# The empty slots of the late expert table moved from its end to its front

## The chip, the cores and the metric

The kernel runs on one core of one Trainium2 chip. Times are device microseconds (us) of one launch. The kernel before takes 1703.07 us, the median of 3 runs (1702.03 to 1703.34). Everything read from a trace comes from one profiled execution.

Names of engines: PE is TensorE, ACT is ScalarE, DVE is VectorE, POOL is GpSimd, SP is SyncE, which only issues DMAs here. Each engine works through its own instructions in order and waits on semaphores.

## The reference, cut to what matters

One decoder layer on x [8, 512, 256], float32: a linear attention, a causal cross attention with 16 heads, and a mixture of 16 experts with the best 4 for each token. The change touches only the last part:

```
def _L0_ffn_ref(hidden_states, router_w, router_b, w1, b1, w2, b2):
    logits = hidden_states @ router_w + router_b
    probs = jax.nn.softmax(logits, axis=-1)
    topw, topi = jax.lax.top_k(probs, 4)
    topw = topw / jnp.sum(topw, axis=-1, keepdims=True)
    combine = jnp.sum(jax.nn.one_hot(topi, 16) * topw[..., None], axis=2)
    ...
    def body(acc, expert):                      # 16 experts
        hmid = jax.nn.gelu(x @ w1e + b1e, approximate=False)
        return (acc + (hmid @ w2e + b2e) * ce[:, None], None)
x = x + _L0_ffn_ref(_layernorm(x), ...)
```

4096 tokens with 4 experts each are 16384 pairs, spread very unevenly over the 16 experts.

## The kernel before, in words

The kernel sorts the pairs by expert in DRAM (`expert_rows`, one region for each expert; a row is the normalised token, its id and its gates) and computes tiles of 256 rows of one expert. How many tiles an expert needs is known only at run time, so the program has a fixed number of slots, `MOE_TILES` = 79, the most that can ever be needed, and a table says for each slot j which expert owns it (`owner`), at which row it starts (`first_row`) and on which earlier slots its output must wait (`landed`).

The table comes in two parts. The first 24 slots (`SURE_TILES`) take full tiles from the first six batches. The other 55 (`LATE_TILES`) are laid out when all tokens are routed: `count_tiles` gives the late tiles of each expert and their running sum `cum`; `find_owners` gives slot n (the column `number`, one slot per partition) the expert whose sums enclose n; `find_rows` turns that into a row and into the two flags `meets`. For the inputs of the reference, counting its routing gives 49 late tiles, for experts 0 to 15:

```
2 1 1 2 1 1 3 1 4 6 1 9 1 1 1 14
```

so 6 of the 55 late slots are empty. An empty slot is computed like any other, on the padding rows that stand behind expert 0's last row; their ids point to 256 spare rows behind the real output. Before the change the real tiles are slots 24 to 72 and the empty ones 73 to 78.

What a slot does, in the order of `attention_plan` (in round j: `turn_x` of j+1, `load_x` of j+3, `hidden` of j, `split_w1` of j+2, `load_w1` of j+4, `results` of j-1):

- SP loads the 256 rows (`load_x`, L1702) and the expert's w1 (`load_w1`, L1721).
- PE transposes the rows (L1739), makes the hidden layer (24 matmuls, L1757) and the results (24 matmuls, L1772).
- DVE copies ids and gates of the rows to `tail` (L1837), of which there are 5 buffers (`NT`): for slot j+1 it first waits until the output of slot j-4 has landed. Behind it stands the low half of the transposed rows (L1839), without which PE can't begin the hidden layer of j+1.
- ACT scales the result with the gate and writes it to `y` (L1805), of which there are 3 buffers (`NY`): it waits until the output of slot j-3 has landed.
- POOL adds the result to the output in DRAM: two indirect DMAs of 128 rows with `compute_op=ADD` (L1874). Two adds in flight must not touch the same output row. Tiles of one expert never do, tiles of two experts can. So POOL waits, before the adds of slot j, for the landing of slot j-1 if j is the first tile of its expert (in this part of the table), and for the landing of slot j-2 if j is its first or second (`meets`, L200; the waits are L1870). From the third tile of an expert on it waits for neither. An empty slot counts as row 0 of its expert, so it waits for both, since all empty slots add to the same spare rows.

The table arithmetic runs on DVE in rounds 8 to 14: `count_tiles` after round 8, `find_owners` after round 10, `find_rows` after round 12, the copy to the tables after round 14.

Of the kernel before, what the change touches and what calls it, by code (L numbers as in the profile page):

```python
# [10 lines left out]
I32 = mybir.dt.int32  # L11
ACT = mybir.ActivationFunctionType
ALU = mybir.AluOpType
AX = mybir.AxisListType

P = 128
# [6 lines left out]
E, TOPK, FF = 16, 4, 512  # L23
# [11 lines left out]
LATE_TILES = MOE_TILES - SURE_TILES  # L35
# [12 lines left out]
class Signal:  # L48


    def __init__(self, nc, stack, name, events, step=1):
        self.sem = stack.enter_context(nc.semaphore(name))
        self.order = list(events)
        self.value = {event: (i + 1) * step for i, event in enumerate(self.order)}
        self.given, self.step = 0, step
# [24 lines left out]
class Phase:  # L80
# [5 lines left out]
    def sb(self, name, shape, dtype=F32):  # L86
        return self.stack.enter_context(self.nc.sbuf_tensor(f"{self.name}_{name}", shape, dtype))
# [49 lines left out]
class Tables:  # L137


    def __init__(self, sb, scr):  # L140
        self.scr, self.scr_i, self.of_tile = scr, sb("scr_i", [P, E], I32), sb("of_tile", [P, 7])

    @staticmethod
    def of_part(part):
        return ["one", "up", "tiles_i", "tiles", *(("less",) if part else ()), "cum", "hit", "owner", "hit_tiles", "before",
                *(("some", "first", "behind", "here", "used", "owner_some") if part else ()), "row",
                *(("row_used",) if part else ()), ("meets", 1), ("meets", 2), *(("row_on",) if part else ()), "row_up", "row_at",
                *(("row_past", "row_some") if part else ("limit", "part_first", "part")),
                "owner_out", "row_out", ("landed", 1), ("landed", 2)]
# [16 lines left out]

    def find_owners(self, dve, w, done, part, number, kept):
        one, tiles, cum, hit = (self.scr[:, i, :] for i in range(4))
        owner, before, row, some, meets_1, meets_2, used = (self.of_tile[:, i:i + 1] for i in range(7))
        mult, add, sub = ALU.mult, ALU.add, ALU.subtract  # L170
        w.wait_ge(done, "cum")
        dve.tensor_scalar(hit, cum, number[:], None, ALU.is_le).then_inc(done.of("hit"), 1)
        w.wait_ge(done, "hit")
        dve.tensor_reduce(owner, hit, AX.X, add).then_inc(done.of("owner"), 1)
        dve.tensor_tensor(tiles, hit, tiles, op=mult).then_inc(done.of("hit_tiles"), 1)
        w.wait_ge(done, "hit_tiles")
        dve.tensor_reduce(before, tiles, AX.X, add).then_inc(done.of("before"), 1)
        if part == 1:
            behind, here = (self.scr[:, i, :] for i in (4, 5))
            dve.tensor_scalar(some, owner, float(E), None, ALU.is_lt).then_inc(done.of("some"), 1)  # L180
            dve.tensor_tensor(behind[:, 0:1], one[:, 0:1], hit[:, 0:1], op=sub).then_inc(done.of("first"), 1)
            dve.tensor_tensor(behind[:, 1:E], hit[:, 0:E - 1], hit[:, 1:E], op=sub).then_inc(done.of("behind"), 1)
            w.wait_ge(done, "behind")
            dve.tensor_tensor(here, behind, kept.used[:], op=mult).then_inc(done.of("here"), 1)
            w.wait_ge(done, "here")
            dve.tensor_reduce(used, here, AX.X, add).then_inc(done.of("used"), 1)
            dve.tensor_tensor(owner, owner, some, op=mult).then_inc(done.of("owner_some"), 1)

    def find_rows(self, dve, w, done, part, number, kept, count):
        cum = self.scr[:, 2, :]  # L190
        owner, before, row, some, meets_1, meets_2, used = (self.of_tile[:, i:i + 1] for i in range(7))
        mult, add, sub = ALU.mult, ALU.add, ALU.subtract
        w.wait_ge(done, "owner_some" if part else "before")
        dve.tensor_tensor(row, number[:], before, op=sub).then_inc(done.of("row"), 1)
        w.wait_ge(done, "row")
        if part == 1:
            dve.tensor_tensor(row, row, some, op=mult).then_inc(done.of("row_used"), 1)
            w.wait_ge(done, "row_used")
        for back, meets in ((1, meets_1), (2, meets_2)):
            dve.tensor_scalar(meets, row, float(back - 1), float(ADD_STEP), ALU.is_le, mult).then_inc(done.of(("meets", back)), 1)  # L200
        w.wait_ge(done, ("meets", 2))
        if part == 1:
            dve.tensor_tensor(row, row, used, op=add).then_inc(done.of("row_on"), 1)
            w.wait_ge(done, "row_on")
        dve.tensor_scalar(row, row, float(ROWS), None, mult).then_inc(done.of("row_up"), 1)
        w.wait_ge(done, "row_up")
        dve.scalar_tensor_tensor(row, owner, float(REGION), row, op0=mult, op1=add).then_inc(done.of("row_at"), 1)
        w.wait_ge(done, "row_at")
        if part == 1:
            dve.tensor_tensor(row, row, count[:, 0:1], op=sub).then_inc(done.of("row_past"), 1)  # L210
            w.wait_ge(done, "row_past")
            dve.scalar_tensor_tensor(row, row, some, count[:, 0:1], op0=mult, op1=add).then_inc(done.of("row_some"), 1)
        else:
            dve.tensor_scalar(cum, cum, float(SURE_TILES), None, ALU.min).then_inc(done.of("limit"), 1)
            w.wait_ge(done, "limit")
            dve.tensor_copy(kept.used[:, 0:1], cum[:, 0:1]).then_inc(done.of("part_first"), 1)
            dve.tensor_tensor(kept.used[:, 1:E], cum[:, 1:E], cum[:, 0:E - 1], op=sub).then_inc(done.of("part"), 1)
# [1765 lines left out]
```

## Time and profile before

| | |
|---|---|
| median of 3 runs | 1703.07 us (1702.03 to 1703.34) |
| the profiled execution | 1697.64 us |
| its span (first to last instruction) | 1695.9 us |
| PE busy | 1592.5 us, 94% of the span |
| POOL busy | 523.8 us, 31% |
| expert rounds | about 1180 to 1695 us of the span |
| one expert round when nothing is late | 6.13 us |

The span is what the views below divide; 1.7 us of the profiled execution's own time lie around it. The views used are the page, the busy time by stretches, the waits, the instructions in order of time on one engine, and the chain of waits (the work that ended last, followed back from the last instruction).

### The profile page before, as it was taken

How to read it: one execution, taken by the hardware profiler on the slowest of the kernel's cores; microseconds unless marked ns; L12 is line 12 of the kernel's file. 1: busy time of each engine (PE TensorE's matmuls, PEld its weight loads, DVE VectorE, ACT ScalarE, POOL GpSimd, SP SyncE). 2: the span in 40 equal slices, each digit the busy share in tenths (PEclk: the TensorE clock that was granted, in tenths of full speed). 3: DMA queues.
4: the chain of work that ended last, by engine and by line, in shares of the span. 5: the costliest groups of instructions: out<-in, count | busy, mean ns of one | idle time of the engine just before them, and what ended most of it. 6: DMA issues, size and time to landing. Idle time of an engine off the chain costs nothing.

```text
span 1695.9 us, 35759 instructions
## 1 busy us (share of the span) xinstructions
PE 1592.5 (94%) x12470; PEld 1338.2 (79%) x12470; DVE 1192.4 (70%) x2751; ACT 1071.8 (63%) x2702; POOL 523.8 (31%) x433
## 2 busy tenths in 40 slices
PE   5899989999999999999999999997989999999995
PEld 4788866777677677677776776775989999999995
DVE  6988957667776677577677767678775665666662
ACT  4555547666666665676666666667666666666663
POOL 2434400000210300301202102106576545654654
PEclk9999989999999999999999999999999999999998
DMA  3122110000110100200200102045699877777763
GB/s 99 38 88 75 38 62 2 1 26 2 46 46 1 60 33 1 72 20 15 78 1 34 58 1 78 15 141 176 155 239 269 198 171 160 183 176 171 183 159 38
DMA packets 94976, 144.54 MB, mean 85 GB/s; under 512 B 12576, under 2 KB 55120, under 8 KB 94800
## 3 DMA queue, kind: packets, MB, share of 16 engines
q1 hardware_dynamic: 64176, 101.40, 19.2%
q0 software_dynamic: 28896, 38.62, 12.0%
q8 instruction: 103, 1.69, 0.4%
q10 hardware_dynamic: 1728, 2.23, 0.4%
q14 instruction: 73, 0.60, 0.1%
HBM read 90.76 MB, written 51.46 MB: 84 GB/s over the span
## 4 chain that ended last, share of the span: by engine, by line
PE 51%; ACT 16%; DVE 10%; issue 4%; DMA 3%; SPq 1%; POOL 1%; POOLq 0%; another core or an unknown queue 0%; DVEq 0%; ACTq 0%
PE ex_H L1757 10%; PE ex_Y L1772 10%; ACT xa_prob L1335 8%; PE xa_work L1250 5%; PE xa_work L1175 5%; PE xa_S L1204 4%; PE xa_work L1186 4%; PE xa_work L1233 4%; PE xa_work L1221 4%; ACT xa_probT L1349 4%; DVE xa_nmax L1453 3%; DMA out<-ex_y,ahead_bits 3%; DVE xa_prob L1465 2%; PE ex_X L1739 2%; DVE xa_q1lo L1446 1%
## 5 line engine op out<-in xcount | busy, mean ns | idle before, releaser
L1335 ACT ACTIVATE xa_prob<-xa_S,xa_nmax 128x512 f32<-128x512 f32 (+3 forms) x512 | 266.4, 535 | 139.2 <-DVE xa_nmax L1453 127.9
L1874 POOL DMA_INDIRECT out<-ex_y,ahead_bits x158 | 263.8, 1670 | 212.0 <-POOLq L1870 82.2
L1757 PE MATMUL ex_H<-ex_xT,ex_w 128*128 128x256 f32 x1896 | 247.4, 287 | 5.2 <-DVE ex_xT L1839 5.2
L1757 PEld LDWEIGHTS ex_H<-ex_xT,ex_w 128*128 128x128 f32 x1896 | 233.1, 192 | 5.6 <-issue 5.6
L1772 PE MATMUL ex_Y<-experts_w_hi,ex_hT 128*128 x1264 | 236.5, 280 | 1.0 <-issue 1.0
L1453 DVE TENSOR_REDUCE xa_nmax<-xa_S 128x2 f32<-128x1024 f32 (+3 forms) x256 | 197.9, 815 | 8.6 <-remote 7.4
L1772 PEld LDWEIGHTS ex_Y<-experts_w_hi,ex_hT 128*128 128x128 f32 x1264 | 198.7, 188 | 1.2 <-issue 1.2
L1626 POOL DMA_INDIRECT expert_rows<-kept_xn,kept_rows x112 | 111.5, 996 | 281.6 <-DVE xa_prob L1465 256.6
L1349 ACT ACTIVATE xa_probT<-xa_work 128x512 f32<-128x512 f32 x256 | 139.8, 602 | 77.9 <-PE xa_work L1221 75.9
L1845 DVE TENSOR_TENSOR ex_hT<-ex_h,ex_hT 128x512 fp32r<-128x512 f32 x158 | 108.7, 692 | 103.5 <-ACT ex_hT L1797 89.9
L1772 PE MATMUL ex_Y<-experts_w_lo,ex_hT 128*128 x632 | 176.3, 279 | 0.0
L1465 DVE TENSOR_SCALAR xa_prob<-xa_prob,xa_sums 128x512 f32<-128x512 f32 (+3 forms) x512 | 169.4, 384 | 6.8
L1221 PE MATMUL xa_work<-ahead_ident,xa_prob 128*128 128x128 f32 x1280 | 159.4, 278 | 9.8 <-DVE xa_prob L1465 6.5
L1805 ACT ACTIVATE ex_y<-ex_Y,ahead_bits 128x256 f32<-128x256 f32 x158 | 66.5, 472 | 156.4 <-PE ex_Y L1772 138.8
L1221 PEld LDWEIGHTS xa_work<-ahead_ident,xa_prob 128*128 128x128 f32 x1280 | 139.7, 142 | 20.9 <-DVE xa_prob L1465 9.3
L1233 PE MATMUL xa_work<-xa_probT,xa_v 128*64 128x512 f32 (+3 forms) x1024 | 153.6, 443 | 0.7 <-ACT xa_probT L1349 0.7
L1792 ACT ACTIVATE ex_h<-ex_H,kept_b 128x256 f32<-128x256 f32 x316 | 132.0, 471 | 12.7 <-PE ex_H L1757 11.7
L1460 DVE RECIPROCAL xa_sums<-xa_sums 128x2 f32<-128x2 f32 (+1 forms) x192 | 32.2, 168 | 144.2 <-ACT xa_prob L1335 144.1
L1233 PEld LDWEIGHTS xa_work<-xa_probT,xa_v 128*64 128x64 f32 x1024 | 68.3, 137 | 81.1 <-issue 67.3
L1772 PEld LDWEIGHTS ex_Y<-experts_w_lo,ex_hT 128*128 128x128 f32 x632 | 118.6, 188 | 0.0
L1335 ACT ACTIVATION_READ_ACCUMULATOR xa_prob<-xa_S,xa_nmax 128x1 f32 x512 | 108.2, 211 | 0.0
L1797 ACT ACTIVATE ex_hT<-ex_h 128x512 fp32r<-128x512 f32 x158 | 100.1, 634 | 5.0
(364 smaller groups left out, 3627.6 us busy)
## 6 DMA issues: line engine op xcount, KB each, us to landing
ex_w_raw<-in_w SPq DMA_DIRECT2D x29, 512.0 KB
kept_x<-expert_rows SPq DMA_DIRECT2D x50, 273.0 KB
ahead_ctx<-in_w SPq DMA_DIRECT2D x25, 512.0 KB
ahead_x<-in_w SPq DMA_DIRECT2D x25, 512.0 KB
kept_xn<-expert_rows SPq DMA_DIRECT2D x29, 273.0 KB
experts_w_lo<-in_w SPq DMA_DIRECT2D x6, 1024.0 KB, 5.8
expert_rows<-ahead_spare SPq DMA_DIRECT2D x32, 136.5 KB
a_x<-in_x SPq DMA_DIRECT2D x8, 512.0 KB, 4.7
```

The source lines that it names most:

```text
L1221: m = pe.transpose(PJ[:, col:col + P], prob[n % 2][:, odd, PROB_AT[i] + j * P:PROB_AT[i] + (j + 1) * P], ident[:])
L1233: m = pe.matmul(OB[HD * odd:HD * odd + HD, j * P:512], v[n % 2][:, j, first_col + HD * odd:first_col + HD * odd + HD], probT[:, odd, PROB_ ...
L1335: m = act.activation(prob[n % 2][:, odd, PROB_AT[i]:PROB_AT[i] + width], SB[slot[at]][:, odd, col:col + width], ACT.Exp, bias=nmax[n % 2][ ...
L1349: act.activation(probT[:, odd, first_col:first_col + 512], bank(step, at)[:], ACT.Copy).then_inc(t_ev.of(at), 1)
L1453: m = dve.tensor_reduce(nmax[n % 2][:, i, :], SB[slot[at]][:, :, SCORE_COL[i]:SCORE_COL[i] + (i + 1) * P], AX.X, ALU.max, negate=True)
L1465: m = dve.tensor_scalar(part, part, sums[n % 2][:, i, odd:odd + 1], None, ALU.mult)
L1626: pool.indirect_dma_start(rows_dram, bass.IndirectOffsetOnAxis(rows_i[b % 2][:, t, k:k + 1], 0), xn3[:, t, :], None).then_inc(scattered[of ...
L1757: m = pe.matmul(bank[:, (f % 2) * ROWS:(f % 2 + 1) * ROWS], ww[:, c, f * P:(f + 1) * P], xx[:, c, :], start=(i == 0), stop=(i == len(terms ...
L1772: m = pe.matmul(bank[:, a * D:(a + 1) * D], hh[:, f, a * P:(a + 1) * P], W2[:, bass.ds(own * WE + f * D, D)], start=(i == 0), stop=(i == l ...
L1792: i = act.activation(h32[:, f, :], HB[2 * (j % 2) + u][:, (f % 2) * ROWS:(f % 2 + 1) * ROWS], ACT.Gelu, bias=b1[j % 2][:, f:f + 1])
L1845: dve.tensor_tensor(hT[j % 2][1][:, fs, :], h32[:, fs, :], f32(hT[j % 2][0][:, fs, :]), op=ALU.subtract).then_inc(h_lo.of((j, u)), 1)
L1874: pool.indirect_dma_start(out, bass.IndirectOffsetOnAxis(tail[j % NT][:, a, 0:1].bitcast(I32), 0), y[j % NY][:, a, :], None, compute_op=AL ...
```

## The change

Slot n of the late table is now read as n minus the number of empty slots: `at` = `cum` of the last expert - 55 + n. For the first 6 late slots `at` is negative, and they are the empty ones; the others follow in the same order as before. So slots 24 to 29 are empty, and the 49 real tiles are slots 30 to 78. The sequence of first, second and further tiles over the slots, written as lengths, is

```
before: 2 1 1 2 1 1 3 1 4 6 1 9 1 1 1 14, six empty
after:  six empty, 2 1 1 2 1 1 3 1 4 6 1 9 1 1 1 14
```

```diff
-        ... self.of_tile = ..., sb("of_tile", [P, 7])
+        ... self.of_tile = ..., sb("of_tile", [P, 8])
     def find_owners(self, dve, w, done, part, number, kept):
         w.wait_ge(done, "cum")
-        dve.tensor_scalar(hit, cum, number[:], None, ALU.is_le).then_inc(done.of("hit"), 1)
+        if part == 1:
+            dve.scalar_tensor_tensor(at, cum[:, E - 1:E], float(-LATE_TILES), number[:], op0=add, op1=add).then_inc(done.of("shift"), 1)
+            w.wait_ge(done, "shift")
+        dve.tensor_scalar(hit, cum, (at if part else number[:]), None, ALU.is_le).then_inc(done.of("hit"), 1)
...
-            dve.tensor_scalar(some, owner, float(E), None, ALU.is_lt).then_inc(done.of("some"), 1)
+            dve.tensor_scalar(some, at, 0.0, None, ALU.is_ge).then_inc(done.of("some"), 1)
     def find_rows(self, dve, w, done, part, number, kept, count):
-        dve.tensor_tensor(row, number[:], before, op=sub).then_inc(done.of("row"), 1)
+        dve.tensor_tensor(row, at if part else number[:], before, op=sub).then_inc(done.of("row"), 1)
```

On the engines only DVE's list of instructions changes. Here is DVE after round 10 (`find_owners` of the late part), before the change; `ahead_bits` holds the scratch of the tables, `ex_of_tile` the columns with one number per slot:

```order
L172 TENSOR_SCALAR ahead_bits<-ahead_bits,ahead_number 128x16 [waits ex_t_dve]
L174 TENSOR_REDUCE ex_of_tile<-ahead_bits 128x1 [waits ex_t_dve]
L175 TENSOR_TENSOR ahead_bits<-ahead_bits 128x16
L177 TENSOR_REDUCE ex_of_tile<-ahead_bits 128x1 [waits ex_t_dve]
L180 TENSOR_SCALAR ex_of_tile<-ex_of_tile 128x1
```

The same place after the change:

```order
L173 SCALAR_TENSOR_TENSOR ex_of_tile<-ahead_bits,ahead_number 128x1 [waits ex_t_dve]
L175 TENSOR_SCALAR ahead_bits<-ahead_bits,ex_of_tile 128x16 [waits ex_t_dve]
L177 TENSOR_REDUCE ex_of_tile<-ahead_bits 128x1 [waits ex_t_dve]
L178 TENSOR_TENSOR ahead_bits<-ahead_bits 128x16
L180 TENSOR_REDUCE ex_of_tile<-ahead_bits 128x1 [waits ex_t_dve]
L183 TENSOR_SCALAR ex_of_tile<-ex_of_tile 128x1
```

One instruction on 128x1 and one wait of DVE on itself have come in; line numbers rise by 3. After round 12 (`find_rows`) DVE began with this row,

```order
L194 TENSOR_TENSOR ex_of_tile<-ahead_number,ex_of_tile 128x1 [waits ex_t_dve]
L197 TENSOR_TENSOR ex_of_tile<-ex_of_tile 128x1 [waits ex_t_dve]
L200 TENSOR_SCALAR ex_of_tile<-ex_of_tile 128x1 [waits ex_t_dve]
```

and now begins with this one:

```order
L197 TENSOR_TENSOR ex_of_tile<-ex_of_tile 128x1 [waits ex_t_dve]
L200 TENSOR_TENSOR ex_of_tile<-ex_of_tile 128x1 [waits ex_t_dve]
L203 TENSOR_SCALAR ex_of_tile<-ex_of_tile 128x1 [waits ex_t_dve]
```

Only an operand differs. The instructions of PE, ACT, POOL and SP stand in the same order; what changes for them are the numbers in the table: which slot reads which rows and which w1, and for which slots POOL waits.

## Rows read from the trace of the kernel before

**Rows 1.** Busy time by stretches: stretch, length, engines' busy us (instructions), PEclk, DMA share, GB/s.

```profile
1437.00:1655.00 218.00, 218.00 (x1850) 218.00 (x1848) 145.82 (x250) 145.29 (x321) 119.95 (x74) 1.00 0.74 173
1655.00:1695.00 40.00, 23.74 (x201) 23.53 (x200) 11.02 (x18) 15.40 (x34) 18.31 (x12) 0.85 0.34 41
```

**Rows 2.** Waits in the expert rounds: us in total, times, longest.

```profile
DVE ahead_bits L1837 <- DMA out<-ex_y,ahead_bits: 19.9, 13, 5.4
```

**Rows 3.** The chain of waits at the end: start us, us, what.

```profile
1656.30 4.84 DMA out<-ex_y,ahead_bits
...
1683.29 3.73 DMA out<-ex_y,ahead_bits
...
1689.76 1.55 POOL out L1874
```

**Rows 4.** POOL in order of time, the end: start us, us, instruction, idle before.

```profile
1654.45 1.54 POOL L1874 DMA_INDIRECT out<-ex_y,ahead_bits  x1 [3.12 <-POOLq L1870]
...
1662.01 1.54 POOL L1874 DMA_INDIRECT out<-ex_y,ahead_bits  x1 [4.17 <-POOLq L1870]
...
1687.91 1.54 POOL L1874 DMA_INDIRECT out<-ex_y,ahead_bits  x1 [3.07 <-POOLq L1870]
```

**Rows 5.** ACT in order of time, the results of slot 77.

```profile
1676.86 0.84 ACT L1805 ACTIVATE ex_y<-ex_Y,ahead_bits 128x256 f32<-128x256 f32 x2 [2.23 <-PE ex_Y L1772]
```

**Rows 6.** ACT and POOL in order of time, slot 72, which waits for no landing.

```profile
1646.34 0.84 ACT L1805 ACTIVATE ex_y<-ex_Y,ahead_bits 128x256 f32<-128x256 f32 x2 [1.87 <-PE ex_Y L1772]
...
1647.94 1.55 POOL L1874 DMA_INDIRECT out<-ex_y,ahead_bits  x1 [2.58 <-ACT ex_y L1805]
```

**Rows 7.** The chain of waits, PE's hidden layers of two successive slots.

```profile
1633.82 2.87 PE ex_H L1757 x24
...
1639.95 2.87 PE ex_H L1757 x24
```

**Rows 8.** POOL in order of time: first adds of slots 24, 26, 27, 28, 29, 30, 32.

```profile
1353.02 1.93 POOL L1874 DMA_INDIRECT out<-ex_y,ahead_bits  x1 [4.10 <-POOLq L1870]
...
1365.35 1.85 POOL L1874 DMA_INDIRECT out<-ex_y,ahead_bits  x1 [3.98 <-issue]
...
1372.20 1.97 POOL L1874 DMA_INDIRECT out<-ex_y,ahead_bits  x1 [3.02 <-POOLq L1870]
...
1381.85 1.54 POOL L1874 DMA_INDIRECT out<-ex_y,ahead_bits  x1 [5.07 <-ACT ex_y L1805]
...
1385.90 1.69 POOL L1874 DMA_INDIRECT out<-ex_y,ahead_bits  x1 [0.31 <-issue]
...
1394.99 1.54 POOL L1874 DMA_INDIRECT out<-ex_y,ahead_bits  x1 [5.55 <-issue]
...
1409.03 2.10 POOL L1874 DMA_INDIRECT out<-ex_y,ahead_bits  x1 [2.99 <-POOLq L1870]
```

**Rows 9.** The chain of waits, 1404 to 1428: landings of slots 31 and 32, PE.

```profile
1404.45 3.70 DMA out<-ex_y,ahead_bits
...
1411.43 6.24 DMA out<-ex_y,ahead_bits
...
1418.80 3.10 PE ex_H L1757 x24
```

**Rows 10.** ACT and DVE in order of time: results of slots 24 and 32, DVE's longest wait.

```profile
1350.08 0.84 ACT L1805 ACTIVATE ex_y<-ex_Y,ahead_bits 128x256 f32<-128x256 f32 x2 [2.04 <-PE ex_Y L1772]
...
1399.07 0.84 ACT L1805 ACTIVATE ex_y<-ex_Y,ahead_bits 128x256 f32<-128x256 f32 x2 [1.96 <-PE ex_Y L1772]
...
1417.76 0.19 DVE L1837 COPY ahead_bits<-kept_x 128x34 f32<-128x34 f32 x1 [5.38 <-DMA out<-ex_y,ahead_bits]
```

**Rows 11.** DVE and PE in order of time, rounds 10 and 12: the price of a small operation, the cover.

```profile
1252.58 0.68 DVE L1839 TENSOR_TENSOR ex_xT<-ex_X,ex_xT 128x512 fp32r<-128x512 f32 x1
...
1264.78 0.20 DVE L207 SCALAR_TENSOR_TENSOR ex_of_tile<-ex_of_tile 128x1 f32<-128x1 f32 x1
...
1255.68 3.11 PE L1757 MATMUL ex_H<-ex_xT,ex_w 128*128 128x256 f32 x24
```

More of the change, by code:

```diff
@@ L140, in __init__ @@
     def __init__(self, sb, scr):
-        self.scr, self.scr_i, self.of_tile = scr, sb("scr_i", [P, E], I32), sb("of_tile", [P, 7])
+        self.scr, self.scr_i, self.of_tile = scr, sb("scr_i", [P, E], I32), sb("of_tile", [P, 8])
     @staticmethod
     def of_part(part):
-        return ["one", "up", "tiles_i", "tiles", *(("less",) if part else ()), "cum", "hit", "owner", "hit_tiles", "before",
+        return ["one", "up", "tiles_i", "tiles", *(("less",) if part else ()), "cum", *(("shift",) if part else ()), "hit", "owner", "hit_tiles", "before",
                 *(("some", "first", "behind", "here", "used", "owner_some") if part else ()), "row",
@@ L168, in find_owners @@
         one, tiles, cum, hit = (self.scr[:, i, :] for i in range(4))
-        owner, before, row, some, meets_1, meets_2, used = (self.of_tile[:, i:i + 1] for i in range(7))
+        owner, before, row, some, meets_1, meets_2, used, at = (self.of_tile[:, i:i + 1] for i in range(8))
         mult, add, sub = ALU.mult, ALU.add, ALU.subtract
         w.wait_ge(done, "cum")
-        dve.tensor_scalar(hit, cum, number[:], None, ALU.is_le).then_inc(done.of("hit"), 1)
+        if part == 1:
+            dve.scalar_tensor_tensor(at, cum[:, E - 1:E], float(-LATE_TILES), number[:], op0=add, op1=add).then_inc(done.of("shift"), 1)
+            w.wait_ge(done, "shift")
+        dve.tensor_scalar(hit, cum, (at if part else number[:]), None, ALU.is_le).then_inc(done.of("hit"), 1)
         w.wait_ge(done, "hit")
@@ L190, in find_rows @@
         cum = self.scr[:, 2, :]
-        owner, before, row, some, meets_1, meets_2, used = (self.of_tile[:, i:i + 1] for i in range(7))
+        owner, before, row, some, meets_1, meets_2, used, at = (self.of_tile[:, i:i + 1] for i in range(8))
         mult, add, sub = ALU.mult, ALU.add, ALU.subtract
         w.wait_ge(done, "owner_some" if part else "before")
-        dve.tensor_tensor(row, number[:], before, op=sub).then_inc(done.of("row"), 1)
+        dve.tensor_tensor(row, at if part else number[:], before, op=sub).then_inc(done.of("row"), 1)
         w.wait_ge(done, "row")
```

## The prediction

> **What bounds the kernel now.** I read the busy time by stretches first: in the long run of expert rounds PE is busy for all of its 218 us, in the last 40 us for 23.7, while POOL goes on [rows 1]. PE's hidden layers follow each other every 6.13 us (1639.95 - 1633.82) [rows 7]. So PE sets the time up to its last slot, and something else sets the rest. The chain of waits says what: over its last 45 us it runs through POOL's adds and their landings alone, 4.84 us for the add issued at 1656.30, 3.73 us for that at 1683.29, and it ends with POOL's last add at 1689.76 [rows 3]. POOL in order of time shows the same: slots 73 to 78 are the empty ones, each waits for the landing of the one before, and their first adds start at 1654.45, 1662.01 and so on to 1687.91 [rows 4].
>
> Then I asked what such a chain costs in the middle. The waits have DVE idle for 19.9 us in 13 places before L1837, the copy that needs a landing 5 slots back [rows 2]. The longest, 5.38 us, ends at 1417.76, and behind it PE begins a hidden layer late, at 1418.80 [rows 9, 10]. So the expert rounds have slack against late adds, and it can be used up.
>
> **What is removed: the tail.** A slot that waits for no landing has its first add 1.60 us after ACT starts its results (slot 72: 1646.34 and 1647.94) [rows 6]. Adds that wait for nothing follow each other after 1.85 us (1687.91 to 1689.76) [rows 3, 4]. After the change the last slots are the 11th to 14th tile of expert 15 and wait for nothing. ACT starts the results of slot 77 at 1676.86 [rows 5]; its adds start at 1678.46 and 1680.31, those of slot 78, whose results are ready by then, at 1682.16 and 1684.01. Before, the last add starts at 1689.76. The tail gets 5.75 us shorter. Its landing I take at the same 3.7 us; if it took the longest of the chain, 6.24 [rows 9], 2.5 us of the gain would go.
>
> **What is moved: six waiting slots into the middle.** Slots 24 to 29 now wait for each other, and behind them come experts 0 to 8 with few tiles each, which wait as well. Call b the time from the start of a slot's results on ACT to its first add. b grows by the step between two first adds minus 6.13.
>
> - A step in which a slot waits for the landing before it, while loads flow: from 1365.35 to 1372.20 it takes 6.85 us, from there to 1381.85 it takes 9.65, and 9.09 from 1385.90 to 1394.99 [rows 8]. There are 17 such steps between slots 23 and 74, the last from 1654.45 to 1662.01, 7.56 us [rows 4]; their mean is 7.68. So b grows by 1.55.
> - A second or later tile behind others: from 1381.85 to 1385.90 [rows 8], 4.05 us; seven such steps average 4.2. b falls by 1.9.
> - The limit. Slot 32: results at 1399.07 [rows 10], second add at 1411.43, landed 6.24 later, at 1417.67 [rows 9]: 18.6 us. PE's hidden layer of slot 37 then starts at 1418.80 [rows 9], where the rhythm of 6.13 would have had 1417.0: 1.8 us late. So up to 16.8 us cost PE nothing. Slot 31, landed at 1408.15 [rows 9], needed 15.2 and cost none. From first add to landing a step has 7.68 less about 0.87 (landing to next first add: 1404.45 + 3.70 to 1409.03 is 0.88) [rows 8, 9], 6.8 us. So b may reach 10.0; what goes beyond is lost by PE, slot for slot.
> - The start. Slot 24: 1353.02 - 1350.08 = 2.94 [rows 8, 10]. It waits before as after.
>
> The sum: b = 2.94, then 4.5, 6.0, 7.6, 9.1 for slots 25 to 28; slot 29 would reach 10.7, so 0.7 is lost; slot 30, first tile of expert 0, loses 1.55; slot 31 relaxes to 8.1. Slots 32 to 34 (experts 1, 2, 3) lose 1.2 + 1.55, slot 35 relaxes; slots 36 to 38 (experts 4, 5, 6) lose 1.2 + 1.55; then expert 6 relaxes to 6.2, and experts 7 and 8 reach 9.3. Together 7.75 us. The averages alone would give no loss before the change (b grows to about 9 there), and yet 1.8 were lost, through one landing of 6.24; I count the same again for such landings after the change. So PE loses 9.5 us in the middle after the change and 1.8 before, 7.7 more. No PE work is there to hide it: PE is busy throughout [rows 1].
>
> The cost of a step inside the new place is the unknown term. Its low end is that of the unloaded tail: four steps from 1662.01 to 1687.91, 6.48 each [rows 4]. Its high end is 9.65 [rows 8]. I take the mean under load, since the six slots now run where loads flow: 173 GB/s in the expert rounds, 41 in the tail [rows 1].
>
> The row on the tail shows 3.73 us without loads and 4.84 with them [rows 3]. The Trainium skill, page "DMA: Bandwidth & Descriptors", section "SWDGE vs HWDGE vs iDMA", says that GpSimd's DMAs and SyncE's feed different queues within each DMA engine, and that the engine takes turns between them. The trace agrees, and by that rule the adds are moved from where they have the engines to themselves to where they share them.
>
> **The added operation.** A SCALAR_TENSOR_TENSOR on 128x1 takes 0.20 us [rows 11], with its wait at most 0.3. It stands in round 10 ahead of DVE's L1837 and L1839. L1839 ends there at 1253.26 and the hidden layer that needs it starts at 1255.68 [rows 11]: 2.4 us of cover, so I count nothing. If the cover were gone it would be 0.3 once. SP and POOL wait for the same copy; nothing of theirs is longer than that either. The changed operand and comparison cost nothing (the same instruction on the same size). Which rows and which w1 an empty slot loads doesn't change its bytes.
>
> **The sum.** - 5.75 + 7.7 = + 2.0 us. Against the profiled execution, 1697.64 (span 1695.9 and 1.7 around it), that is 1699.6. The median of the runs is 5.4 above the profiled execution, so the forecast for the median is 1703.07 + 2.0 = 1705.1 us.
>
> **Rivals.** A: the empty slots' adds land fast in the middle too, 6.48 us a step, since all go to one compact block of 256 spare rows. For it: four steps of the tail. Against it: the one step of the tail that ran while loads flowed took 7.56 [rows 4]. b is then 5.0 at slot 30, and the whole run up to slot 38 loses 0.7, with one long landing perhaps 2: the time is 5.75 less and little else, about 1697.5. The Trainium skill, same page, section "Anatomy of one DMA — SWDGE (gpsimd) path", gives about 2.0 us plus bytes over 436 GB/s, an estimate of 2.3 us for an add of 128 KB. With 2.3 in place of 3.7 or 4.9 a step would take some 5 us, b would never grow, and the change would be gain alone, as in A; the landings of 3.73 to 6.24 speak against it [rows 3, 9].
>
> B: the steps in the saturated stretch are longer than the mean, 8.2 us. Before the change the five such steps between 1365.35 and 1409.03 average 7.9, with two of 9.65 and 9.09 among them [rows 8], and that is where the experts with few tiles already ran late. When DVE waits for a landing, the tail copy, the next row load and the next adds all start at once behind it, and meet at the DMA engines. Then b grows by 2.07 a step up to 9.5, slots 28 to 30 lose 5.9, slots 32 to 38 lose 8.6, experts 7 and 8 another 0.3: 14.8, or 13 more than before; + 7.2 gives 1710.3. The verdict turns at a step of about 7.8 us: each 0.1 costs 1.3 us.
>
> C: the table comes out with the same order of slots. The arithmetic speaks against it: `at` is negative for exactly the first six. 1703.1.
>
> **Chances.** A measurement of this kernel tells 0.2%, 3.4 us, from no change: faster is below 1699.7, slower above 1706.5. The forecast's case has 0.55, within ±4 us of 1705.1; A 0.13, B 0.30, C 0.02. Faster: A and little else, 0.15. Within: most of the forecast's case, and C, 0.43. Slower: B and the forecast's upper part, 0.42. The range for 8 in 10 leaves out most of A and the end of B: 1699.0 to 1712.0. The likeliest case's own range is 1701 to 1709.
>
> **What would show it.** In the changed kernel's trace the last landing follows PE's last results by about 7 us, and the chain of waits runs over PE to the end, POOL adding only its last few issues. Between 1352 and 1400 POOL's first adds are 6.9 to 9.6 us apart for 14 slots with two or three relaxations; the waits of DVE before L1840 (L1837 before) grow from 19.9 to over 50 us; PE stands idle before L1760 (hidden layer) about nine times 1 us between 1385 and 1450. The forecast is wrong if the first adds of slots 24 to 30 stand 6.5 us apart (A) or over 8 (B), if PE has more slack than 16.8 us, or if the last adds still wait for landings.

## The result and the profile after

The changed kernel takes 1709.55 us, the median of 20 runs (1702.45 to 1717.89), against 1702.22 for the kernel before (1694.02 to 1707.83): ratio 1.0050, 95% interval 1.0037 to 1.0063. It is slower, by 7.3 us from median to median; the interval of the ratio is 6.3 to 10.7 us. The forecast was 1705.1 with a range of 1699.0 to 1712.0; rival B had 1710.3. The profiled execution took 1709.30 us with a span of 1707.5, 11.6 us more than the one of before. Of these, 3.5 us lie ahead of slot 24, where the kernels do the same work (its results start at 1353.53 against 1350.08); this start isn't fixed (a second profiled execution of the changed kernel, on another chip, has it at 1344.23), so I compare from slot 24 on. The other 8.1 us are 13.8 more in slots 24 to 77 and 5.7 less in the tail, as the next views show.

The busy time of PE on the page of the changed kernel, which is 7 us longer for the same 12470 matmuls:

```profile
PE 1599.7 (94%) x12470; PEld 1344.0 (79%) x12470; DVE 1192.0 (70%) x2752; ACT 1072.7 (63%) x2702; POOL 526.8 (31%) x433
```

Busy time by stretches of the changed kernel (stretch, length, PE, PEld, DVE, ACT, POOL, PEclk, DMA share, GB/s):

```profile
1345.00:1380.00 35.00, 35.00 (x298) 35.00 (x298) 23.77 (x41) 22.99 (x52) 16.51 (x10) 1.00 0.69 169
1380.00:1470.00 90.00, 80.98 (x658) 80.14 (x657) 49.11 (x86) 52.30 (x115) 48.52 (x27) 0.96 0.67 153
...
1670.00:1707.00 37.00, 26.02 (x220) 25.81 (x219) 12.19 (x22) 17.60 (x39) 18.55 (x12) 0.89 0.38 45
```

PE is without work for 9 of the 90 us from 1380 to 1470, where it lacked none before but 1.6 us, and its granted clock falls there (0.96). The last 37 us answer to [rows 1].

The end of the chain of waits of the changed kernel, which answers to [rows 3], and the last results on ACT, which answer to [rows 5]:

```profile
1690.36 5.67 PE ex_Y L1775 x48
...
1699.45 1.55 POOL out L1877
...
1701.30 1.55 POOL out L1877
```

```profile
1694.14 0.84 ACT L1808 ACTIVATE ex_y<-ex_Y,ahead_bits 128x256 f32<-128x256 f32 x2 [2.22 <-PE ex_Y L1775]
1696.69 0.84 ACT L1808 ACTIVATE ex_y<-ex_Y,ahead_bits 128x256 f32<-128x256 f32 x2 [1.70 <-PE ex_Y L1775]
```

The chain now runs over PE up to its last matmul, then over three adds that follow each other every 1.85 us, with no landing between. From the results of slot 77 to the end of the span it is 1707.5 - 1694.1 = 13.4 us; before, 1695.9 - 1676.9 = 19.0 [rows 5]. The tail got 5.7 us shorter.

The middle: from the results of slot 24 to those of slot 77 there are 53 rounds, 325.2 us at 6.135 each. Before they took 326.8 (1350.08 to 1676.86), after it 340.6 (1353.53 to 1694.14). I call what is over 325.2 PE's loss: 1.6 before, 15.5 after. POOL in order of time over slots 24 to 30 of the changed kernel, first adds (answers to [rows 8]):

```profile
1355.95 1.54 POOL L1877 DMA_INDIRECT out<-ex_y,ahead_bits  x1 [3.87 <-POOLq L1873]
...
1369.49 1.94 POOL L1877 DMA_INDIRECT out<-ex_y,ahead_bits  x1 [3.20 <-issue]
...
1378.82 1.54 POOL L1877 DMA_INDIRECT out<-ex_y,ahead_bits  x1 [4.79 <-ACT ex_y L1808]
1380.67 2.04 POOL L1877 DMA_INDIRECT out<-ex_y,ahead_bits  x1 [0.30 <-issue]
1386.64 1.54 POOL L1877 DMA_INDIRECT out<-ex_y,ahead_bits  x1 [3.93 <-POOLq L1873]
1388.49 1.83 POOL L1877 DMA_INDIRECT out<-ex_y,ahead_bits  x1 [0.30 <-issue]
1393.20 2.44 POOL L1877 DMA_INDIRECT out<-ex_y,ahead_bits  x1 [2.88 <-POOLq L1873]
1395.94 2.30 POOL L1877 DMA_INDIRECT out<-ex_y,ahead_bits  x1 [0.30 <-issue]
1403.38 1.74 POOL L1877 DMA_INDIRECT out<-ex_y,ahead_bits  x1 [5.14 <-issue]
```

1355.95 is slot 24, 1403.38 slot 30: 47.4 us for six steps, 7.9 each, where PE needs 36.8. The lag piles up as forecast, and then the waits of the expert rounds answer to [rows 2] (engine, what it waited for, us in total, times, longest):

```profile
DVE ahead_bits L1840 <- DMA out<-ex_y,ahead_bits: 39.5, 14, 5.6
...
ACT ex_y L1808 <- DVE ahead_bits L1840: 20.9, 6, 4.6
...
PE ex_H L1760 <- DVE ex_xT L1842: 14.2, 6, 3.7
```

The longest of PE's six, 3.7 us, stands before the hidden layer of slot 1, long ahead of the change, and is there in the kernel before too (3.6). The other five come to some 10.5 us: 1.2, 3.1, 1.5, 3.2 and 1.5 before slots 34, 35, 42, 43 and 70.

What I had not forecast stands in PE's own rows. PE in order of time, changed kernel, the hidden layers of slots 34, 35 and 43:

```profile
1403.28 3.11 PE L1760 MATMUL ex_H<-ex_xT,ex_w 128*128 128x256 f32 x24 [1.21 <-DVE ex_xT L1842]
...
1412.78 5.46 PE L1760 MATMUL ex_H<-ex_xT,ex_w 128*128 128x256 f32 x24 [3.12 <-DVE ex_xT L1842]
...
1469.66 4.60 PE L1760 MATMUL ex_H<-ex_xT,ex_w 128*128 128x256 f32 x24 [3.24 <-DVE ex_xT L1842]
```

The same 24 matmuls take 3.11 us, 5.46 and 4.60. The stretches around the second one show why:

```profile
1403.20:1409.40 6.20, 6.12 (x52) 6.15 (x52) 3.14 (x5) 3.83 (x9) 5.41 (x3) 1.00 0.49 102
1409.40:1412.70 3.30, 0.26 (x3) 0.02 (x1) 0.95 (x3) 0.34 (x1) 1.72 (x2) 0.87 0.99 194
1412.70:1418.30 5.60, 5.52 (x26) 5.55 (x27) 4.34 (x8) 2.48 (x7) 3.53 (x2) 0.50 0.38 70
```

After 3.1 us without work PE's granted clock is 0.50, the 1.2 GHz level, while it works again. In the hidden layers alone that costs 5.46 - 3.11 = 2.35 us here and 4.60 - 3.11 = 1.49 there, 3.8 of the 15.5.

### The profile page after: what moved, and what is told of

Read it like the earlier page. It is cut to its first block, busy times and chain, and to the rows that moved or that the text cites. A ratio compares the mean times of both kernels' runs of the same rounds, so it can differ in the third digit from the quotient of the medians.

```text
span 1707.5 us, 35760 instructions
## 1 busy us (share of the span) xinstructions
PE 1599.7 (94%) x12470; PEld 1344.0 (79%) x12470; DVE 1192.0 (70%) x2752; ACT 1072.7 (63%) x2702; POOL 526.8 (31%) x433
## 4 chain that ended last, share of the span: by engine, by line
PE 48%; ACT 16%; DVE 10%; DMA 5%; issue 5%; SPq 1%; POOL 1%; POOLq 1%; another core or an unknown queue 0%; ACTq 0%; DVEq 0%
PE ex_H L1760 9%; PE ex_Y L1775 8%; ACT xa_prob L1338 8%; PE xa_work L1253 5%; PE xa_work L1178 5%; DMA out<-ex_y,ahead_bits 5%; PE xa_S L1207 4%; PE xa_work L1189 4%; PE xa_work L1236 4%; PE xa_work L1224 4%; ACT xa_probT L1352 3%; DVE xa_nmax L1456 3%; DVE xa_prob L1468 2%; PE ex_X L1742 1%; POOL out L1877 1%
## 5 line engine op out<-in xcount | busy, mean ns | idle before, releaser
L1760 PE MATMUL ex_H<-ex_xT,ex_w 128*128 128x256 f32 x1896 | 252.3, 291 | 14.2 <-DVE ex_xT L1842 14.2
L1760 PEld LDWEIGHTS ex_H<-ex_xT,ex_w 128*128 128x128 f32 x1896 | 238.0, 196 | 15.5 <-issue 15.5
```

The costliest lines, as they stand in the source:

```text
L1760: m = pe.matmul(bank[:, (f % 2) * ROWS:(f % 2 + 1) * ROWS], ww[:, c, f * P:(f + 1) * P], xx[:, c, :], start=(i == 0), stop=(i == len(terms ...
```

## The experiments

All kernels of one call ran on one chip, beside the kernel before; chips differ by some 15 us in the time ahead of slot 24, so only ratios are compared between calls. PE's loss (slots 24 to 77, as above) and the tail (results of slot 77 to the end of the span) come from one profiled execution each. Lag, from here on, is the time from the end of a slot's results on ACT to its first add, 0.84 us less than the b of the prediction: the changed kernel's largest lag, 12.5 us, is a b of 13.3.

| kernel | ratio to before, 95% interval | PE's loss | tail |
|---|---|---|---|
| before | 1 | 1.6 | 19.0 |
| changed | 1.0050, 1.0037 to 1.0063 | 15.5 | 13.4 |
| changed, again | 1.0047, 1.0030 to 1.0065 | 15.2 | 13.3 |
| operation alone | 0.9994, 0.9978 to 1.0009 | 1.7 | 19.4 |
| empty in front, no waits | 0.9977, 0.9958 to 0.9996 | 5.2 | 13.5 |
| empty at the end, no waits | 0.9952, 0.9934 to 0.9970 | 1.1 | 13.3 |
| six within the last expert | 0.9991, 0.9974 to 1.0007 | 5.5 | 13.4 |
| one by one in the last expert | 0.9973, 0.9959 to 0.9987 | 1.4 | 13.5 |
| three in front | 1.0019, 0.9997 to 1.0040 | 6.1 | 13.5 |
| before, quarter of w1 | 0.9979, 0.9962 to 0.9996 | -0.1 | 20.8 |
| changed, quarter of w1 | 1.0018, 1.0004 to 1.0032 | 7.4 | 13.4 |
| changed, next to no loads | 0.9959, 0.9940 to 0.9978 | -0.1 | 13.6 |
| changed, one buffer more | 0.9997, 0.9979 to 1.0014 | 7.2 | 13.0 |
| before, one tail buffer less | 1.0180, 1.0154 to 1.0207 | 21.8 | 20.3 |

**The added operation alone.** `at` is made equal to the slot's number, the order stays that of before:

```diff
-            dve.scalar_tensor_tensor(at, cum[:, E - 1:E], float(-LATE_TILES), number[:], op0=add, op1=add)
+            dve.scalar_tensor_tensor(at, cum[:, E - 1:E], 0.0, number[:], op0=mult, op1=add)
-            dve.tensor_scalar(some, at, 0.0, None, ALU.is_ge)
+            dve.tensor_scalar(some, owner, float(E), None, ALU.is_lt)
```

> The order of the slots of before, with only the added DVE instruction and its wait. Theory W (the waiting slots in the middle cost the time): no change against before, ratio 1.000 within 0.002, since the instruction takes 0.2 us beside 2.4 us of cover. Rival D (the longer chain of table arithmetic costs it): about as slow as the changed kernel, 7 us or 0.4% over before.

Measured: 1688.04 us against 1689.88, ratio 0.9994. No change that can be told, and its slots 24 to 77 together take the time of before within 0.1 us. The operation is not the cause.

**Empty slots in front, without waits.** The flags of the empty slots say "third tile", and each adds to spare rows of its own:

```diff
-            dve.tensor_tensor(row, row, some, op=mult)
+            dve.scalar_tensor_tensor(row, some, -8.0, row, op0=mult, op1=add)
-            dve.tensor_scalar(meets, row, float(back - 1), float(ADD_STEP), ALU.is_le, mult)
+            dve.tensor_scalar(meets, row, float(back - 1 - 8 * part), float(ADD_STEP), ALU.is_le, mult)
...   # the 8 is added back before the row is scaled
-                    pool.indirect_dma_start(out, ..., y[j % NY][:, a, :], None, compute_op=ALU.add)
+                    pool.indirect_dma_start(out, ..., y[j % NY][:, a, :], None, element_offset=own_spare, compute_op=ALU.add)
```

> The six empty slots stand in front as in the changed kernel, but wait for no landing: each adds to 256 spare rows of its own behind the output, and its flags say so. Theory W: the loss in the middle falls to that of before (1 to 2 us), the shorter tail stays, so about 5.7 us under before (1696.5 for a before of 1702.2, ratio 0.9967) and 13 under the changed kernel. Rival P (the place of the empty slots costs it whatever they wait for, by other rows and another w1 at the DMA engines): as slow as the changed kernel, 7 us over before.

Measured: 1686.24 against 1689.88, ratio 0.9977; the changed kernel had 1.0050 and 1.0047, each on its own chip. So what the six slots wait for is worth about 0.7%, 12 us, and rival P falls. (The rows that they add to were changed along with the waits, not apart from them.) It was expected at 0.9967, inside the interval; its profile shows a loss of 5.2 us where 1 to 2 were expected. I followed the real slots one by one: the lag of experts 0 to 3 is that of before within 0.8 us (2.2, 3.1, 6.1 us at the first tiles of experts 1, 2 and 3, against 2.3, 2.7, 6.5), and then four landings of 6.2 to 6.8 us within six slots (33 and 36 to 38) lift it to 12.8, where before it peaked at 9.1 with two such landings around; 1.5 us of the 5.2 are again a hidden layer at half clock (4.60 us). One execution can't say whether this place always draws them.

**Empty slots at the end, without waits.** The order of before; in `find_rows` the flag column gets 2 added for empty slots, and the adds of slots 73 to 78 have spare rows of their own:

```diff
-            dve.tensor_tensor(row, row, some, op=mult)
+            dve.scalar_tensor_tensor(row, self.scr[:, 3, E - 1:E], 2.0, row, op0=mult, op1=add)
```

> The order of before, the six empty slots at the end, but each with spare rows of its own and no wait. Theory W: the tail alone gets shorter, by 5.7 us (ratio 0.9967), and PE's loss in the middle stays as before; same time as with the free slots in front. Rival P: same as theory W here, but 13 us faster than the free slots in front.

Measured: 1682.62 against 1689.88, ratio 0.9952, the lowest of all, though its interval overlaps those of several others. Expected was 0.9967, in the interval at its edge. The tail is 13.3 us, that of the changed kernel to 0.1. So the gain of 5.7 us that the change was credited with is real, and the waits of the last six slots are what it removes. Its slots are written down for this routing, so as it stands it is a measurement and not a version for other inputs.

**Six waiting slots within the last expert.** Seven more small DVE operations (eight in, one out) choose the place:

```diff
+            dve.tensor_scalar(some, at, float(42), None, ALU.is_ge)        # behind the gap
+            dve.tensor_tensor(at, at, some, op=mult)
+            ...                                                           # meets_1: ahead of the gap
+            dve.tensor_tensor(some, some, meets_1, op=add)
```

> The six empty slots wait as in the changed kernel, but stand within the 14 tiles of the last expert: slots 66 to 71, with 7 real tiles behind them that wait for nothing. Theory W: the tail is short (-5.7 us), the six waiting slots start from a lag of 0.8 us and gain 1.6 to 1.8 each, which the slack nearly holds, so PE loses 1 to 3 us there: about 3 to 5 us under before, 1697 to 1699, ratio 0.997 to 0.998. Rival P or a rival by which any waiting slot under load costs PE its 1.6 us at once: 6 x 1.6 = 10 us lost, 4 us over before.

Measured: 1688.86 against 1689.88, ratio 0.9991. The tail is short, but PE lost 5.5 us, 1.5 of it at slots 35 and 36 as before and 3.9 at slots 73 to 75, behind the six. So six waiting slots in a row use up the slack even from a lag of 0.8 us: the lag reached 13.6. Rival P's number, + 4 us, is outside the interval. The time alone doesn't tell this kernel from before; theory W's loss of 1 to 3 us was too small, the profile has 3.9.

**One by one in the last expert.** The same, but the six empty slots take every second place from slot 63 on (some 17 small DVE operations; the places are computed from the number of empty slots, so this one isn't tied to the routing, but by its arithmetic it holds for at most eight empty slots, and only six were run):

```diff
+            dve.tensor_scalar(self.scr_i[:, 0:1], number[:], float(-39), None, add)
+            dve.tensor_scalar(self.scr_i[:, 0:1], self.scr_i[:, 0:1], 1, None, ALU.arith_shift_right)
+            ...   # place = 39 + half for odd, empty for even; behind them number - empties
```

> The six empty slots wait as in the changed kernel, but stand one by one between real tiles of the last expert (slots 63, 65, ... 73; real tiles between and four behind). Some 17 small DVE instructions more in rounds 8 and 10. Theory W: each empty slot adds 1.6 to the lag and each real one takes 1.9 away, so PE loses nothing there, and the tail is short: 5 to 6 us under before, ratio 0.9967; up to 1 us of this can go to the longer table arithmetic. Rival: the step of a waiting slot costs PE by itself, then 4 us over before.

Measured: 1687.13 against 1692.12, ratio 0.9973 (0.9959 to 0.9987), as expected, with a loss of 1.4 us, all at slots 35 and 36 where before has it too. Beside it, in the same call, the changed kernel itself:

> The changed kernel itself beside the lean kernels and the interleaved one. Theory W: 7 us over before (ratio 1.004), with PE's loss in slots 24 to 77 between 10 and 16 us and 13.4 us from the results of slot 77 to the end of the span (19.0 before).

Measured: 1701.68 against 1692.12, ratio 1.0047, loss 15.2, tail 13.3: the result holds on another chip. The same six waiting slots cost 13.8 us of PE in front of experts 0 to 8 and nothing between tiles that wait for nothing.

**Three in front, three in the last expert.**

```diff
+            dve.tensor_scalar(meets_1, number[:], float(3), None, ALU.is_ge)      # slots 24 to 26 empty
+            ...                                                                  # gap of three at slots 69 to 71
```

> Three empty slots in front of the late ones (24 to 26), three within the last expert (69 to 71, 7 real tiles behind them); all wait. Theory W: the first three bring the lag to 5 or 6 us before expert 0 comes, so PE loses 4 to 6 us, about half of what six cost; with the short tail the time is 1 to 3 us under before. Rival: the loss goes with the number of waiting slots under load, wherever they stand; then as e4, 1 us under before.

Measured: PE's loss is 6.1 us, as expected (4 to 6), 1.5 of it through a clock of 0.50 for one hidden layer of 4.59 us. The time is 1706.96 against 1705.40, ratio 1.0019 (0.9997 to 1.0040), not the 1 to 3 us under before; a loss of 6.1 and a tail of 13.5 would give 1 us under. The difference stays open. Part of it may lie ahead of slot 24, whose results start at 1360.3 here and at 1358.2 and 1360.8 in two other kernels on the same chip; one execution of each can't tell.

**A quarter of w1.** Both orders, with 128 KB of w1 loaded from slot 26 on in place of 512:

```diff
-                sp.dma_start(w1_raw[buffer_of[j]], d['w1'][...]
+                part = (slice(0, P), slice(0, KC)) if j < SURE_TILES + 2 else (slice(0, P // 2), slice(0, 1))
+                sp.dma_start(w1_raw[buffer_of[j]][part[0], part[1], :], d['w1'][...][part[0], part[1], :]
```

> The order of before, but from slot 26 on each slot loads a quarter of its w1 (128 KB in place of 512 KB; the rest of the buffer holds older weights). Theory L (the landing of an add is long when the w1 load meets it at the DMA engines): landings all near 3.8 to 4.3 us, steps of 6.5 to 6.9, no loss of PE in the middle, 1 to 2 us under before. Rival S (landings are long by themselves, by the scattered rows of the output): landings over 6 us stay, time as before.

> The changed order with the same quarter loads of w1. Theory L with W: steps of 6.5 to 6.9 don't use up the slack, PE loses 0 to 2 us in the middle, the short tail is left: 5 to 6 us under before with quarter loads, 13 under the changed kernel. Rival S: PE still loses over 10 us in the middle, 7 us over before with quarter loads.

Measured: before 1689.94 against 1692.12 (0.9979), changed 1694.81 (1.0018). The loss of the changed order fell from 15.5 to 7.4, not to 0 to 2. The runs are less clear: the difference between the two orders fell from 9.6 to 4.9 us by medians, but from 0.47% to 0.39% by ratios whose intervals overlap, and by loss and tail alone the two would now be level (7.4 us more loss, 7.4 less tail). In the profiled executions the 5.2 us between them lie ahead of slot 24, where the orders don't differ. Landings over 5.9 us nearly vanished (from 9 of 50 to 1), but eleven of 5.0 to 5.3 stand where the changed kernel has three. Theory L was half the truth: a second load was left, the 273 KB of rows.

**Next to no loads.** The changed order, with 4 KB of w1 from slot 26 and only the 17 columns of ids and gates of the rows from slot 28:

```diff
-                sp.dma_start(x_in[buffer_of[j]][:], rows_dram[...]
+                cols = slice(0, PAY) if j < SURE_TILES + 4 else slice(D, PAY)
+                sp.dma_start(x_in[buffer_of[j]][:, :, cols], rows_dram[...][:, :, cols]
```

> The changed order, but late slots load next to nothing: 4 KB of w1 from slot 26 on, and of the rows only ids and gates (17 of 273 columns) from slot 28 on; the adds are whole. With a quarter of w1 the loss only halved (15 to 7 us), so either the row loads do the rest (theory L2: landings 3.7 to 4.0, steps 6.5, no loss of PE, 6 us or more under before) or a landing is long for another reason than bytes in flight, such as any DMA issued by SP 1.7 us after the add (rival: steps of 8 to 9 remain, loss of PE over 5 us).

Measured: 1698.81 against 1705.40, ratio 0.9959 (0.9940 to 0.9978), 6.6 us under before. Busy time by stretches of this kernel:

```profile
1350.00:1470.00 120.00, 120.00 (x1019) 120.00 (x1019) 80.64 (x138) 79.32 (x176) 64.41 (x39) 1.00 0.42 48
1470.00:1670.00 200.00, 200.00 (x1696) 200.00 (x1696) 132.97 (x228) 133.60 (x295) 105.32 (x66) 1.00 0.42 48
```

and its wait that answers to [rows 2]:

```profile
DVE ahead_bits L1843 <- DMA out<-ex_y,ahead_bits: 2.4, 1, 2.4
```

With 48 GB/s in place of 153 to 173 PE has no gap at all in these stretches, with the same waits of POOL in the same slots. The mean step of a waiting slot is 6.8 us (22 of them) against 7.8 in the changed kernel. So the loads make the steps long, and at 6.8 the slack holds. This is the strongest of the experiments for the whole chain of the argument: same order, same waits, loss gone, tail kept. (The order of before was not run with these loads.)

**One buffer more.** The changed order with 4 result and 6 tail buffers (`NY, NT = 4, 6`, the fourth result buffer in a tile that is free by then):

```diff
-NY, NT = 3, 5
+NY, NT = 4, 6
+        y.append(ahead.xn[:, 0:RT, :])
+        tail = [*tail, sb("tail5", [P, RT, PAY - D])[:]]
```

> The changed order with one more buffer each for results (4) and tails (6), so that landings may come one round (6.13 us) later before ACT or DVE wait. Theory W (the late adds cost through these buffers alone): the lag of slots 24 to 42 grows as in the changed kernel or further, but PE loses 0 to 5 us there in place of 15; time 2 to 5 us under before. Rival T (the adds disturb PE in another way, by traffic or a slower clock): loss as in the changed kernel, 8 us over before.

Measured: 1705.43 against 1705.40, ratio 0.9997. The lag grew to 18.3 us (12.5 in the changed kernel), as it may with one more round of slack, and the loss fell from 15.5 to 7.2. Its waits:

```profile
DVE ahead_bits L1842 <- DMA out<-ex_y,ahead_bits: 17.5, 6, 5.4
...
PE ex_H L1762 <- DVE ex_xT L1844: 8.2, 3, 4.0
```

Of PE's three waits the 4.0 is again the one of slot 1. The late adds reach PE through these buffers. One round of slack wasn't enough for the pile; I expected a loss of 0 to 5 and a time 2 to 5 us under before.

**One tail buffer less.** The order of before with `NY, NT = 3, 4`.

> The order of before with 4 tail buffers in place of 5: DVE waits for a landing one round earlier, so the slack of 16.8 us falls to 10.7. Theory W: slots 26 to 37 and 56 to 60 now lose time, 10 to 14 us in all, 1.006 to 1.008. Rival: the slack isn't set by this buffer but by the 3 result buffers, then no change.

Measured: 1736.11 against 1705.40, ratio 1.0180, 30.7 us slower. Its waits:

```profile
DVE ahead_bits L1837 <- DMA out<-ex_y,ahead_bits: 149.9, 66, 6.1
...
PE ex_H L1757 <- DVE ex_xT L1839: 16.1, 8, 3.6
```

(The 3.6 is again slot 1's.) The loss in slots 24 to 77 is 21.8 us, twice what I expected. The 24 slots ahead of them take 169.3 us against 160.3 before (158.6 to 165.0 in the other kernels), which my estimate left out. The direction is clear: this buffer's wait bounds the slack.

## Why the prediction was right, and where it was off

The time lies in the stated range and on the side that was forecast, but it is 0.5 us outside the range of 1701 to 1709 given for the likeliest case, and by the prediction's own bounds the forecast was "within" and the result is "slower".

**The tail** was right: forecast - 5.75 us, measured - 5.7 (19.0 to 13.4), and the same 13.0 to 13.6 in every kernel whose last slots don't wait. The landing of the last add stayed short.

**The added operation** was right: nothing.

**The middle** had the right mechanism and was the mis-sized term: forecast 7.7 us more than before (9.5 against 1.8), measured 13.8 (15.5 against 1.6). That the mechanism is this one is shown from four sides: without the waits of the empty slots the cost goes (1.0050 to 0.9977), with one more buffer it halves, with one less the kernel before slows by 1.8%, and without loads it vanishes. The place was right in part. The forecast lost time behind slots 29 and 30, 32 to 34 and 36 to 38, about nine times 1 us; PE's five gaps are behind the adds of slots 29 and 30 (1.2 and 3.1 us), 37 and 38 (1.5 and 3.2) and, not forecast, 65 (1.5). DVE's waits came to 39.5 us, not to over 50. The size was off for two reasons.

First, the step. I took 7.68 us for a waiting step, the mean over the kernel before (7.62 with the step to slot 73, 6.51, which also waits and was left out). In the changed kernel slots 24 to 30 average 7.9, between my figure and rival B's 8.2; over all 22 waiting steps the mean is 7.8, with 7 over 8.5 us where before there were 2 of 17. My own sentence that each 0.1 of it costs 1.3 us was the warning: 0.2 more makes 2.6. B's reason for long steps, that loads and adds start together behind a landing, is supported by when they occur. SP in order of time in the changed kernel, beside two landings of its chain of waits:

```profile
1391.85 0.38 SPq L1724 DMA_DIRECT2D ahead_x<-in_w  x1
1393.39 0.33 SPq L1705 DMA_DIRECT2D kept_x<-expert_rows  x1
1397.63 0.36 SPq L1724 DMA_DIRECT2D ex_w_raw<-in_w  x1
```

```profile
1388.49 3.84 DMA out<-ex_y,ahead_bits
...
1395.94 6.21 DMA out<-ex_y,ahead_bits
```

DVE and POOL in order of time around the second:

```profile
1394.87 0.69 DVE L1829 CAST ex_w<-ex_w_raw 128x1024 fp32r<-128x1024 f32 x1
1395.59 1.23 DVE L1831 TENSOR_TENSOR ex_w<-ex_w_raw,ex_w 128x1024 fp32r<-128x1024 f32 x1
...
1395.94 2.30 POOL L1877 DMA_INDIRECT out<-ex_y,ahead_bits  x1 [0.30 <-issue]
```

The add issued at 1388.49 has the next w1 load 3.4 us behind it and lands in 3.84 us. The one at 1395.94 has it 1.7 us behind and needs 6.21. In slots 24 to 71 of the changed kernel there are eight second adds with the w1 load 1.7 us behind, and all of them need between 6.2 and 6.5 us; of the 14 with the load 3 to 4 us behind, 13 land in 3.8 to 4.5. One other landing is as long (slot 64), with the load 0.6 us ahead. In the kernel before five adds have the load 1.7 us behind and need 6.1 to 7.0, and three others are nearly as long (5.9 to 6.2). In a steady round the load comes 4.1 us behind and misses them. As the lag grows, the adds slide over the round, and once in each pass they meet the load, which adds some 2.4 us at one stroke. The average hid that.

The load alone doesn't make the 2.4 us. In all eight cases POOL's second add starts 0.4 us after the CAST (L1829) has ended, its instruction takes 2.30 us where 1.55 is usual, and SP issues the w1 load 0.8 us after L1831, which frees the buffer. So the 1.7 us are no chance: both hang on the same two DVE instructions. Such an add with no w1 load behind it (slots 70 and 71 of "six within the last expert") lands in 4.5 and 4.3 us against 3.8 of the usual ones without loads; with 4 KB behind it needs 4.4 to 5.3 (three cases), with 128 KB mostly 5.0 to 5.3 (nine of ten), with 512 KB 6.2 to 6.5. Some 0.5 to 0.7 us thus come with the longer instruction and the rest with the size of the load. That DVE is what holds POOL up is read from the times; no run moved its instructions.

Second, a term that the forecast did not have: PE's clock. After two gaps of about 3 us it worked at half clock for a while, which cost 3.8 us in all (above); not every such gap does this (last section). Before the change the one hidden layer that started late, by 1.8 us, took 3.10 as usual [rows 9]. Without it the middle would have lost 11.7, against a forecast of 9.5.

So the number was low by 4.5 us, within its range, and the direction was right; between my case (0.55) and B (0.30) the measurement is B's: a forecast + 7.2, measured + 7.3, though B reached it without the clock and with a longer step than there was, so that its hit is luck in part.

One rule that I weighed, from the Trainium skill, page "DMA: Bandwidth & Descriptors", section "SWDGE vs HWDGE vs iDMA" (queues of GpSimd and SyncE take turns within a DMA engine): the prediction had the trace agree, and it does in that adds and loads get in each other's way, with mean steps of 7.8, 7.4 and 6.8 us as the loads of a slot go from 785 to 401 to about 21 KB. It doesn't agree that they take turns: in the eight long adds the w1 load's packets come first (from 2.7 us behind the add's start on), and at most 10 of the add's 144 packets come before four fifths of the load's 256 are through. The measurement decides. The fit of the Trainium skill, same page, section "Anatomy of one DMA — SWDGE (gpsimd) path", an estimate of 2.3 us for such an add, is not what was measured: the shortest landings are 3.5 us here, in tails without loads, counted from the start of POOL's instruction, which takes 1.55 of them.

## What to carry to other kernels

Waiting work at the end of a kernel costs its waits once, openly; moved to where transfers flow, each wait gets longer, and a run of them costs nothing until the slack of the buffers is used up and everything after that. So before moving such work, count the slack in buffers, the gain in lag of each step, and what stands behind it: here the same six slots cost 13.8 us in front of nine experts that also wait, 3.9 in a row before free tiles, and nothing one by one between free tiles (0.9973 of before). And look for the waits themselves: giving the six empty slots rows of their own removed them and had the lowest ratio (0.9952), though its interval, 0.9934 to 0.9970, overlaps that of one by one, 0.9959 to 0.9987.

## What was not expected of the hardware

- PE's granted clock fell to 0.50 (1.2 GHz level) after a gap of 3.12 us within an otherwise full stretch, so that 24 matmuls took 5.46 us in place of 3.11; after gaps of 3.24 and 2.97 us they took 4.60 and 4.59. The length of the gap alone doesn't decide it: before the change, 1.8 us late, they took 3.10 [rows 9], in the kernel with free empty slots in front 4.60 after a gap of 1.85, with the quarter loads no gap of up to 2.0 us had this effect, and with one buffer more not even this one of 3.08:

```profile
1476.22 3.11 PE L1762 MATMUL ex_H<-ex_xT,ex_w 128*128 128x256 f32 x24 [3.08 <-DVE ex_xT L1844]
```

  Where it comes, a stall of 3 us costs 4.5 to 5.5.
- An indirect add of 128 rows of 1 KB lands mostly in 3.5 to 5.4 us, but in 6.2 to 6.5 when a 512 KB load is issued 1.7 us behind it. The delay is at the start. Where POOL's instruction takes 1.55 us and nothing is in the way, the add's first packet comes 2.1 us after its start; where it takes 2.30 us, 2.9, with no load, 4 KB or 128 KB behind it; in the eight cases with 512 KB behind it, 4.5 to 4.8, when most of the load's packets, which began at 2.7, are through. In two other executions a 512 KB load began only at 3.4, behind the add's first packet at 2.9, and there 106 and 109 of the add's 144 packets came before four fifths of the load's. So it matters which of the two begins first, and here POOL's extra 0.75 us decided it; the latter is my estimate from 2.1, 2.7 and 2.9, and no run tests it.
